# Cross attention on one Trainium2 core: eight heads' maxima subtracted inside ScalarE's exponentials, score products of two sequences side by side on TensorE, the join a slot later, and no loop

## The reference

```python
query = seq2 + b_self                       # seq2 = side input, seq1 = x
key   = concat([seq1 + b_prev, seq2 + b_self]);  value = concat([seq1, seq2])
q, k, v = query @ Wq + bq, key @ Wk + bk, value @ Wv + bv      # 16 heads of 8
score_prev = einsum('bhqd,bhkd->bhqk', q, k[:, :, :l1]) * SCALE
score_self = (q * k[:, :, l1:]).sum(-1, keepdims=True) * SCALE
score_prev = where(mask, score_prev, -inf)                     # by seq_len1
weights = softmax(concat([score_prev, score_self], -1))
attn = weights[..., :-1] @ v[:, :, :l1] + weights[..., -1:] * v[:, :, l1:]
return attn @ Wo + bo
```

## Time and profile before

| | |
|---|---|
| median of three runs | 5659.84 us (5644.22 to 5665.61) |
| the profiled execution | 5666.48 us, its span 5664.7 us |
| mean granted PE clock over the span | 0.938 |
| busy over the span: PE, DVE, ACT, POOL | 88%, 66%, 59%, 55% |
| first join (L2410) of the block, last join | 5131.27 us, 5472.87 us |

### The profile page before, as it was taken

The page is one execution under the profiler, slowest core; times in us unless marked ns, Lnnn a source line. Parts: engine busy times, 40 slices in busy tenths (PEclk is TensorE's granted clock), DMA queues, the critical chain, the costliest instruction groups (busy, mean ns, idle before and its releaser), DMA issues. The chain is left out here.

```text
span 5664.7 us, 139636 instructions
## 1 busy us (share of the span) xinstructions
PE 4998.9 (88%) x49540; PEld 3198.4 (56%) x49552; DVE 3738.3 (66%) x6448; ACT 3349.9 (59%) x10268; POOL 3134.2 (55%) x1457
## 2 busy tenths in 40 slices
PE   5998999457599999999999999999999999978864
PEld 1333778244366655666566656665666566634532
DVE  2111000754288968886788778876888689847888
ACT  0000000333189968996799769985999499934432
POOL 0001000112399948995799669975998499920018
PEclk9999999659699999999999999999999999988975
DMA  7767554022100000000000000000000000000000
GB/s 157 224 176 202 116 109 101 4 64 54 39 2 2 2 17 6 2 2 17 6 2 2 17 6 2 2 16 7 2 2 2 21 2 2 2 24 7 7 2 14
DMA packets 274391, 204.00 MB, mean 36 GB/s; under 512 B 179524, under 2 KB 254756, under 8 KB 267588
## 3 DMA queue, kind: packets, MB, share of 16 engines
q1 hardware_dynamic: 192924, 114.18, 8.7%
q10 hardware_dynamic: 78760, 76.68, 4.7%
q0 software_dynamic: 2048, 4.20, 0.3%
HBM read 131.83 MB, written 63.16 MB: 34 GB/s over the span
## 5 line engine op out<-in xcount | busy, mean ns | idle before, releaser
L1835 POOL TENSOR_TENSOR rs<-ss,minus_half 128x16 f32<-128x16 f32 x386 | 1128.1, 2923 | 106.8 <-DVE ss L1904 102.5
L1752 ACT ACTIVATE s_ps<-s_ps,low 128x128 f32<-128x128 f32 x3072 | 1059.8, 349 | 4.5
L1833 POOL TENSOR_TENSOR t<-t 128x1024 f32<-128x1024 f32 x386 | 912.2, 2363 | 128.8 <-DVE t L1893 128.8
L1840 POOL TENSOR_TENSOR qk<-t,rs 128x1024 f32<-128x1024 f32 x386 | 735.0, 1904 | 60.4 <-POOL rs L1835 23.7
L1752 ACT ACTIVATION_READ_ACCUMULATOR s_ps<-s_ps,low 128x1 f32 x3072 | 660.3, 215 | 0.0
L1887 DVE TENSOR_TENSOR t<-qk_ps,rot 128x1024 f32<-128x1024 f32 x386 | 472.3, 1224 | 178.4 <-PE qk_ps L1534 178.2
L1915 DVE TENSOR_REDUCE low<-s_ps 128x4 f32<-128x512 f32 x768 | 494.4, 686 | 123.4 <-PE s_ps L1569 122.8
L1924 DVE TENSOR_TENSOR p<-s_ps,rec 128x512 f32<-128x512 f32 x768 | 531.0, 691 | 27.0
L343 PE MATMUL l_ps<-l_core 9*128 9x512 bf16 x4096 | 443.0, 628 | 77.5 <-DMA l_core<-rows_xs 67.3
L1596 PEld LDWEIGHTS att_oT_ps<-pT,v 128*64 128x64 f32 x6144 | 328.6, 137 | 286.6 <-issue 286.6
L1766 ACT ACTIVATE pT<-pT_ps 128x512 f32<-128x512 f32 x768 | 457.1, 595 | 52.4 <-PE pT_ps L1575 43.8
(11 more groups left out here) (400 smaller groups left out, 8560.5 us busy)
## 6 DMA issues: line engine op xcount, KB each, us to landing
l_core<-rows_xs SPq DMA_DIRECT2D x512, 72.0 KB
rows_hs<-l_core ACTq DMA_DIRECT2D x96, 384.0 KB, 6.5
z_fm<-rows_hs SPq DMA_DIRECT2D x120, 144.0 KB
x_fm<-rows_hs SPq DMA_DIRECT2D x120, 144.0 KB
wqkv<-in_wqkv SPq DMA_DIRECT2D x7, 1536.0 KB, 6.5
l_core<-rows_exs ACTq DMA_DIRECT2D x320, 18.0 KB
rows_xs<-z_fm ACTq DMA_DIRECT2D x12, 384.0 KB, 7.5
rows_exs<-l_near ACTq DMA_DIRECT2D x9, 512.0 KB, 11.7
```

The costliest lines, as they stand in the source:

```text
L1752: ins = act.activation(s_ps[:, e, i * P:(i + 1) * P], s_ps[:, e, i * P:(i + 1) * P], ACT.Exp, bias=low[:, c % 2, e, i:i + 1], scale=-1.0, ...
L1833: pool.tensor_tensor(t1[:, i, :], t1[:, i, :], t2[:, i, :], ALU.add).then_inc(s_["t12"], 1)
L1835: pool.tensor_tensor(rs[:, i, :], ss[:, i, :], R.minus_half[:, 0:2 * UH], ALU.pow).then_inc(s_["rs"], 1)
L1840: pool.tensor_tensor(qk[:, i, :].rearrange("p (h d) -> p h d", d=DH), t1[:, i, :].rearrange("p (h d) -> p h d", d=DH), rs[:, i, :].unsquee ...
```

## The change

- DVE's subtraction of the maxima of the high heads goes. DVE computes `minus` = -SCALE times the eight maxima (128x8), and ACT takes eight exponentials of 128x128 out of `s_ps`, each with one column of `minus` as its bias. The low heads keep their subtraction; `z_` has one half.
- The high scores, their maxima and exponentials move a slot later (lag 6); on PE they stand directly ahead of the low scores of the next unit.
- The turns of the high half, the values, the own weight, join, output and finish move a slot later too (7 or 8), `keep_p` is split into two halves, `pT` has two sets of four and `vz` four. The quantiser's stages move a slot later.
- Join goes to the head of DVE's slot, and finish behind both halves' maxima.
- `pipeline` with period equal to units writes all slots as straight code.

```diff
+    if period == units:
+        for s in range(units + lag):
+            for f, g in stages:
+                if 0 <= s - g < units:
+                    f(k0 + s - g, s - g, s - g)
+        return
...
-                pipeline(pool, B, 2 * GS, [(copy_x, 0), (products, 2), (own_value, 6)])
+                pipeline(pool, B, B, [(copy_x, 0), (products, 2), (own_value, 8)])
...
-                    pe.wait_ge(s_["z"], at((k - 1) * 2 + half))
+                    if half:
+                        pe.wait_ge(s_["exh"], at(k - 1))
+                    else:
+                        pe.wait_ge(s_["z"], at(k - 1))
...
-                    pe.wait_ge(s_["ex"], at(k * 2 + g // 2))
+                    pe.wait_ge(s_["exh"] if g // 2 else s_["exl"], at(k))
...
-                pipeline(pe, B, 2 * GS, [(first, 5), (turn_low, 6), (second, 5), (turn_high, 6),
-                                         (project, 1), (output, 7), (values, 6)])
+                pipeline(pe, B, B, [(turn_high, 7), (values_in, 5), (turn_low, 6), (scores_high, 6), (scores_low, 5),
+                                         (output, 8), (project, 1), (values, 7)])
...
                 def exp_high(k, j, c):
-                    exps(k, 1)
+                    act.wait_ge(s_["minus"], at(k))
+                    act.wait_ge(s_["pT"], at((k - 1) * 4 + 3))
+                    for n in range(8):
+                        ins = act.activation(p[:, 1, n * S:(n + 1) * S], s_ps[:, 2 + n // 4, n % 4, :], ACT.Exp,
+                                             bias=minus[:, c % 2, n:n + 1], scale=SCALE)
+                    ins.then_inc(s_["exh"], 1)
...
-                pipeline(act, B, 2 * GS, [(own_copy, 5), (keep_p, 6), (exp_low, 5), (projected, 1), (exp_high, 5),
-                                          (own_weight, 6)])
+                pipeline(act, B, B, [(own_weight, 8), (keep_high, 7), (keep_low, 6), (own_copy, 5), (exp_high, 6),
+                                          (exp_low, 5), (projected, 1)])
...
+                def attend_high(k, j, c):
+                    n, t, scores = halves(k, c, 1)
                     row_max(k, c, 1)
+                    own_max(k, c, 1)
+                    dve.wait_ge(s_["exh"], at(k - 2))
+                    dve.tensor_scalar(minus[:, c % 2, :], t, -SCALE, None, ALU.mult).then_inc(s_["minus"], 1)
                     dve.wait_ge(s_["owe"], at(k - 1))
                     dve.tensor_tensor(ownz[:, :], own[:, c % 2, :], top[:, c % 2, :], ALU.subtract
                                       ).then_inc(s_["ownz"], 1)
...
-                pipeline(dve, B, 2 * GS, [(keep_v, 5), (shift, 0), (attend_low, 5), (join, 7), (max_high, 5), (finish, 7),
-                                          (attend_high, 5), (keys, 2), (masks, 4), (block_scales, 8), (block_values, 9), (block_bins, 10),
-                                          (block_round, 11)])
+                pipeline(dve, B, B, [(join, 8), (keep_v, 5), (attend_high, 6), (attend_low, 5), (finish, 8),
+                                          (shift, 0), (keys, 2), (masks, 4), (block_scales, 9), (block_values, 10),
+                                          (block_bins, 11), (block_round, 12)])
```

More of the change, by code:

```diff
@@ L2073, in level3_cond @@
         mrow = m.sb("ca_mrow", [P, 2, S], BF16)
-        vz = m.sb("ca_vz", [P, 2, GT])
+        vz = m.sb("ca_vz", [P, 4, GT])
         own = m.sb("ca_own", [P, 2, CH])
@@ L2078, in level3_cond @@
         oweb = m.sb("ca_oweb", [P, 2, P])
-        z_ = m.sb("ca_z", [P, 2, 2 * GT])
+        z_ = m.sb("ca_z", [P, 2 * GT])
+        minus = m.sb("ca_minus", [P, 2, 8])
         p = m.sb("ca_p", [P, 2, 2 * GT])
-        pT = m.sb("ca_pT", [P, 4, GT])
+        pT = m.sb("ca_pT", [P, 8, GT])
         owe = m.sb("ca_owe", [P, 2, P])
@@ L2101, in level3_cond @@
         names = ("init", "lens", "onez", "x", "xs", "pr", "prc", "k4", "prod", "mrow", "v", "vc", "ownc", "sc",
-                 "top", "topo", "z", "ex", "ownz", "owe", "pT", "pTc", "oweT", "od", "owec", "t", "den", "rec",
+                 "top", "topo", "z", "minus", "exl", "exh", "ownz", "owe", "pT", "pTc", "oweT", "od", "owec", "t", "den", "rec",
                  "num", "att", "y", "yc", "xstep", "xq")
@@ L2109, in diagonal @@
         def diagonal(c):
-            a = vz[:, c % 2, :]
+            a = vz[:, c % 4, :]
             return bass.AP(a.tensor, a.offset, [a.ap[0], [4 * 32, 4], [32 + CD, 4], [1, CD]])
@@ L2131, in load @@
                     sp.dma_start(side[:, i, :], T["side"][:, bass.ds(j * S, GT)]).then_inc(side_in[i], 16)
-                pipeline(sp, B, 2 * GS, [(load, 0)])
+                pipeline(sp, B, B, [(load, 0)])
             @block.gpsimd
@@ L2229, in values @@
                             v = (4 * g + h) * 32
-                            pe.matmul(o_ps[32 * g:32 * g + 32, 0, :], vz[:, c % 2, v:v + 32],
-                                      pT[:, g, h * S:(h + 1) * S], start=h == 0, stop=h == 3, skip_group_check=True)
+                            pe.matmul(o_ps[32 * g:32 * g + 32, 0, :], vz[:, c % 4, v:v + 32],
+                                      pT[:, 4 * (c % 2) + g, h * S:(h + 1) * S], start=h == 0, stop=h == 3, skip_group_check=True)
                     for h in range(4):
@@ L2234, in values @@
                             mm = pe.matmul(o_ps[32 * g:32 * g + 32, 1, :], onez[:, h * 32:h * 32 + 32],
-                                           pT[:, g, h * S:(h + 1) * S], start=False, stop=h == 3,
+                                           pT[:, 4 * (c % 2) + g, h * S:(h + 1) * S], start=False, stop=h == 3,
                                            skip_group_check=True)
@@ L2241, in output, with scores_high, scores_low @@
                     pe.matmul(o_ps[:, 2, :], att[:, c % 2, :], wo[:, :], start=True, stop=True).then_inc(s_["y"], 1)
-                def first(k, j, c):
-                    values_in(k, j, c)
+                def scores_high(k, j, c):
+                    scores(k, c, 1)
+                def scores_low(k, j, c):
                     scores(k, c, 0)
-                def second(k, j, c):
-                    scores(k, c, 1)
                 def turn_low(k, j, c):
@@ L2288, in own_copy, with keep_p, keep_low, keep_high @@
                     act.activation(own[:, c % 2, :], m_ps[:, P:P + CH], ACT.Copy).then_inc(s_["ownc"], 1)
[L2290 to L2299, removed]
+                def keep_p(k, c, g):
+                    act.wait_ge(s_["pT"], at(k * 4 + g))
+                    act.wait_ge(s_["od"], at(k - 2))
+                    act.activation(pT[:, 4 * (c % 2) + g, :], pT_ps[g % 2][:, :], ACT.Copy).then_inc(s_["pTc"], 1)
+                def keep_low(k, j, c):
+                    keep_p(k, c, 0)
+                    keep_p(k, c, 1)
+                def keep_high(k, j, c):
+                    keep_p(k, c, 2)
+                    keep_p(k, c, 3)
                 def exp_low(k, j, c):
-                    exps(k, 0)
+                    act.wait_ge(s_["z"], at(k))
+                    act.wait_ge(s_["pT"], at((k - 1) * 4 + 1))
+                    act.activation(p[:, 0, :], z_[:, :], ACT.Exp, bias=0.0, scale=SCALE).then_inc(s_["exl"], 1)
                 def exp_high(k, j, c):
-                    exps(k, 1)
+                    act.wait_ge(s_["minus"], at(k))
[4 more added lines that the diff above has]
+                    ins.then_inc(s_["exh"], 1)
                     act.wait_ge(s_["ownz"], at(k))
@@ L2333, in keep_v @@
                     dve.wait_ge(s_["v"], at(k))
-                    dve.wait_ge(s_["od"], at(k - 2))
+                    dve.wait_ge(s_["od"], at(k - 4))
                     dve.tensor_tensor(diagonal(c), m_ps[:, 0:P].rearrange("p (g h d) -> p g h d", g=4, h=4),
@@ L2374, in row_max, with own_max @@
                     dve.tensor_reduce(t, scores, AX.X, ALU.max).then_inc(s_["top"], 1)
-                def less_max(k, c, half):
+                def own_max(k, c, half):
                     n, t, scores = halves(k, c, half)
@@ L2380, in less_max, with attend_low @@
                     dve.wait_ge(s_["topo"], at(n))
-                    dve.wait_ge(s_["ex"], at(n - 2))
-                    dve.tensor_tensor(z_[:, half, :].rearrange("p (h k) -> p h k", h=8), scores,
+                def attend_low(k, j, c):
+                    n, t, scores = halves(k, c, 0)
+                    row_max(k, c, 0)
+                    own_max(k, c, 0)
+                    dve.wait_ge(s_["exl"], at(k - 1))
+                    dve.tensor_tensor(z_[:, :].rearrange("p (h k) -> p h k", h=8), scores,
                                       t.unsqueeze(2).to_broadcast([P, 8, S]), ALU.subtract).then_inc(s_["z"], 1)
[L2385 to L2389, removed]
+                def attend_high(k, j, c):
+                    n, t, scores = halves(k, c, 1)
                     row_max(k, c, 1)
-                def attend_high(k, j, c):
-                    less_max(k, c, 1)
+                    own_max(k, c, 1)
```

(2 more changed lines are left out.)

## The result

The changed kernel took 5717.1 us (median of 4 runs, 5698.6 to 5722.7) against 5656.1 us for the kernel before (4 runs): ratio 1.0101, 95% interval 1.0076 to 1.0126. Run once more beside the experiments, it took 5697.0 us (8 runs) against 5660.2 (25 runs): ratio 1.0059, interval 1.0037 to 1.0081, 33 us by that ratio. It is slower.

What follows compares the result with a forecast made beforehand. A ring of waits between DVE and PE, no full engine, was taken as the bound. Slots from 11.44 to 12.5 over 27 gave 28.6, plus 6 and 6: 40.6 us on 5666.5, 5707; for the median 5700, range 5645 to 5738.

Steps and rivals of the forecast that it cites:

- The ring: DVE and PE waiting on each other within a slot, from values through both maxima to finish: 10.85 us at full clock.
- POOL's share: In one slot of four, join waits for POOL's product and delays DVE's high maximum 1.05 us, 0.26 a slot.
- The clock: PE's wait ahead of the own weights' turn lowers its clock in every slot: 1.4 us, giving a slot of 12.5.
- the paired case: On PE, low scores run beside high ones, leaving PE idle 3.6 us in one piece; 2.4 if not paired.
- The clock holds: Rival: PE's clock stays up in the block, the slot is 11.1 us, the time 5662, no change; chance 0.25.
- DVE's work bounds: Rival: DVE's side work fills its waits, so the slot follows its work: 9.4 us, 5617 in all; chance 0.11.
- Eight exponentials: On ACT, eight exponentials take 2.8 us against 1.06 for the one before, off the ring, adding nothing.
- Filling and last joins: At the block's two ends: one slot more before the first join, 6 us, and longer last four joins, 6 us.
- The sum: Whole kernel: 28.6 us over 27 slots plus 6 plus 6, 40.6 us slower.
- The signs: Expected in the block's profile: joins 12 to 13 us apart, 15 in each fourth slot, granted clock below 0.8.
- the 11.44: Average slot in us of the kernel before, its two loop turns included, against which the forecast slot was compared.

Runs made afterwards that it cites:

- the kernel with the wait filled: The changed kernel with ten products that nobody reads on PE between project and values: 5644.6 us, ratio 0.9982.
- the fastest kernels: The changed kernel with finish between the two halves on DVE, 5621.3 us; the same with the own value's product first on POOL too, 5612.9 us.
- the three kernels with the loop: The kernel before; the kernel before with only the eight biased exponentials, 5655.7 us; the changed kernel with its slots in a loop of 8 again, 5719.2 us.
- finish moved: The changed kernel with finish between the high and the low half on DVE instead of behind both: 5621.3 us, ratio 0.9914.

## Why the prediction was right

It gave 5700 us with a range of 5645 to 5738, slower with 0.54; the two measurements are 5717 and 5697.

- *The ring.* Right in every member. Its full-clock length was put at 10.85, and 11.1 with POOL's share; the kernel with the wait filled has 10.48 in a slot without POOL's share and 10.57 on average. Of the 0.37, two comparisons make 0.18 (0.20 each for 0.29) and the high turn 0.10 (0.93 for 1.03).
- *The clock.* Right in its mechanism, small by a fifth in its size: 1.4 us a slot forecast, 1.71 measured by filling the wait. Values alone make 1.3 of it (3.45 for 2.14); the rest lies in the turns behind, where a fall lasts longer. That these two errors, 0.5 and 0.3, nearly cancel is luck: slot 12.5 forecast, 12.28 measured. The wait was 3.3 us for 3.6, so the paired case held. The Trainium skill (TensorE: Matmul & The Clock Gate, HAM oscillation — how this bites in real kernels) describes a wait that comes back in every round and throttles the array each time; the trace agrees, with 27 waits and a clock of 0.82.
- *The rivals.* "The clock holds" gave 5662; the kernel in which it holds took 5644.6, no change within what can be told. "DVE's work bounds" needed finish not to sit behind the low subtraction, and gave a slot of 9.4 and 5617 us. The kernel in which just that was changed has 9.49 and 5621. The number is near by luck, since what the rival named isn't what sets that slot: DVE has 8.33 us of work in it, and the light slots have the 9.32 of the ring through ACT's exponential and `projected`, which the prediction doesn't have.
- *Eight exponentials.* 2.17 us for eight, 382 ns one, against the 2.8 taken; off the ring, as said: the same eight stand in the fastest kernels. The Trainium skill (ScalarE: Activation LUTs, What ACT_TABLE_LOAD costs) came nearer: from its figures I estimate 2.35 us for eight, and 387 ns for one alone.
- *Filling and last joins.* 6 and 6 forecast, 7.0 and 7.1 measured.
- *POOL.* The wait of 2.06 us is there. 0.26 a slot was forecast, 7 us in 27 slots; with the wait filled a fourth slot is 0.75 longer than the others, 0.19 a slot, and turning POOL's order took 6.3 us from the block.
- *The sum.* 40.6 us forecast, 36.8 in the block. The first median, 61 us above before, holds more than that; the second, 37, fits.
- *The signs.* Clock below 0.8 in the block: 0.80. Joins 12 to 13 us apart and 15 in each fourth slot: 11.2 to 12.9, 14.2 to 14.8 in the fourth, and 10.5 to 10.9 behind it, which I had not seen.
- *Missed:* that the straight code alone is worth 12 to 16 us of the block; I had it only as part of the 11.44 that I compared with. And the remedy, one stage moved, was in the text as a rival's condition and not as the thing to look at.

## What to carry to other kernels

Taking work off an engine that isn't full may earn nothing; find the ring of waits, and put the consumer that frees a buffer as early in its queue as its input allows. Then look for the next ring before calling the busiest engine the bound: an engine busy in 88% of a slot wasn't it here. The same 1.2 us instruction was worth nothing that could be told in one order and all of itself in another. A saving on TensorE that only lengthens one wait can cost more than it saves, when that wait brings the clock down: look at how PE's idle time is cut into pieces, not at its sum.

## What the runs showed of the hardware

- Score products from four strips of 32 rows, two of one sequence and two of another, run side by side: 12 instructions in the time of 6, 1.19 us against 1.18.
- Ten products that nobody reads (20 instructions on PE), 2.39 us a slot, made a block of 427 us 52 us shorter.
- The turn of the loop cost PE 2.5 to 4.1 us of issue time twice in a block, in the three kernels with the loop; the 27 slots of the kernel before and of the changed one as straight code had none. Issue in the list of waits is no proof by itself: the 1.2 us booked so in each slot with finish moved end just behind a copy of ACT's.
- The stretch ahead of the block, the same in all kernels, varies by some 50 us between profiled executions (first transfer from 5057 to 5105 us); a change of 37 us is better read from its block than from four runs of the whole.
